# The slot softmax of a gated-slot attention: eight biased exponentials with their row sums, in place of one exponential over a shifted copy

## The reference, cut to what matters

```
z  = cumlogsumexp(s);  g = exp(z_prev - z);  p = exp(s - z)
hk = hk * g + k (x) p          ok = q . hk      # 64 slot scores per token and head
pv = softmax(ok, axis=-1)                       # over the 64 slots: the part that is changed
hv = hv * g + p (x) v          ov = pv . hv
o  = ov * rsqrt(mean(ov^2) + 1e-5) * g_norm_weight * silu(gate);  out = o @ Wo
```

## Time and profile before

| | |
|---|---|
| median of three runs | 2185.8 us |
| the profiled execution's own time | 2185.81 us |
| its span (first to last instruction) | 2184.1 us |
| TensorE (PE) matrix products busy | 2024.7 us, 93% of the span |
| VectorE (DVE) busy | 1399.1 us, 64% |
| ScalarE (ACT) busy | 671.1 us, 31% |
| GpSimd (POOL) busy | 282.9 us, 13% |
| mean granted TensorE clock | 0.976 of full speed |

### The profile page before, as it was taken

The page is one execution under the profiler, slowest core; times in us unless marked ns, Lnnn a source line. Parts: engine busy times, 40 slices in busy tenths (PEclk is TensorE's granted clock), DMA queues, the critical chain, the costliest instruction groups (busy, mean ns, idle before and its releaser), DMA issues. The chain is left out here.

```text
span 2184.1 us, 30684 instructions
## 1 busy us (share of the span) xinstructions
PE 2024.7 (93%) x11728; PEld 1665.3 (76%) x11728; DVE 1399.1 (64%) x2579; ACT 671.1 (31%) x1156; POOL 282.9 (13%) x243
## 2 busy tenths in 40 slices
PE   0999999969999999999999999999998489999996
PEld 0888888857887878878878878788877368888885
DVE  6665656767666666666666666666677556665666
ACT  2443444534121121212221221212221134443443
POOL 4000000131021020120110110201111220000004
PEclk9999999979999999999999999999999689999999
DMA  5433334430010010000100100100001152432336
GB/s 205 142 122 101 132 104 142 145 121 23 1 37 8 1 38 8 18 28 1 37 9 1 37 8 1 37 8 18 20 1 39 58 145 94 136 126 96 126 126 241
DMA packets 46932, 149.61 MB, mean 69 GB/s; under 512 B 5856, under 2 KB 5856, under 8 KB 46816
## 3 DMA queue, kind: packets, MB, share of 16 engines
q1 hardware_dynamic: 38544, 121.13, 17.2%
q0 software_dynamic: 8272, 26.76, 3.7%
HBM read 125.83 MB, written 22.04 MB: 68 GB/s over the span
## 5 line engine op out<-in xcount | busy, mean ns | idle before, releaser
L1154 PE MATMUL at_pj<-at_w_lo,at_xT_hi 128*128 128x512 f32 x512 | 209.7, 410 | 0.0
L1154 PE MATMUL at_pj<-at_w_hi,at_xT_hi 128*128 128x512 f32 x512 | 201.4, 393 | 0.0
L1154 PE MATMUL at_pj<-at_w_hi,at_xT_lo 128*128 128x512 f32 x512 | 200.4, 391 | 0.0
L1128 PE MATMUL at_pj<-at_xT_hi,at_w_lo 128*128 128x512 f32 x384 | 160.4, 418 | 12.2 <-issue 11.5
L503 DVE TENSOR_TENSOR first_ff_w_lo<-first_ff_stage,first_ff_w_hi 128x1024 fp32r<-128x1024 f32 x80 | 98.0, 1226 | 100.7 <-ACT first_ff_w_hi L365 100.7
L503 DVE TENSOR_TENSOR last_ff_w_lo<-last_ff_stage,last_ff_w_hi 128x1024 fp32r<-128x1024 f32 x80 | 98.0, 1224 | 96.8 <-ACT last_ff_w_hi L365 96.5
L1128 PE MATMUL at_pj<-at_xT_lo,at_w_hi 128*128 128x512 f32 x384 | 153.1, 399 | 0.0
L1128 PE MATMUL at_pj<-at_xT_hi,at_w_hi 128*128 128x512 f32 x384 | 153.0, 398 | 0.0
L773 POOL TENSOR_TENSOR at_coef<-at_ms,minus_half 128x4 f32<-128x4 f32 x64 | 63.6, 1010 | 558.5 <-DVE at_ms L1088 558.5
L749 POOL TENSOR_TENSOR at_w_lo<-at_stage,at_w_hi 128x1024 fp32r<-128x1024 f32 (+1 forms) x36 | 78.5, 2180 | 396.7 <-ACT at_w_hi L813 396.7
L1108 DVE TENSOR_TENSOR xres<-at_r,xres 128x512 f32<-128x512 f32 x128 | 88.2, 689 | 64.8 <-PE at_r L1308 64.1
(11 more groups left out here) (284 smaller groups left out, 4774.6 us busy)
## 6 DMA issues: line engine op xcount, KB each, us to landing
first_ff_stage<-wff SPq DMA_DIRECT2D x80, 512.0 KB, 3.3
last_ff_stage<-wff SPq DMA_DIRECT2D x80, 512.0 KB
at_stage<-watt SPq DMA_DIRECT2D x24, 512.0 KB, 3.6
at_stage<-watt SPq DMA_DIRECT2D x16, 384.0 KB, 3.3
xres<-x SPq DMA_DIRECT2D x4, 1024.0 KB, 10.1
first_ff_xg<-sorted_rows SPq DMA_DIRECT2D x4, 1024.0 KB, 7.2
slot_rows<-first_ff_y POOLq DMA_DIRECT2D x4, 1024.0 KB, 5.3
last_ff_xg<-sorted_rows SPq DMA_DIRECT2D x4, 1024.0 KB, 8.2
```

The costliest lines, as they stand in the source:

```text
L1128: last = pe.matmul(PJ[(7 * k + part) % 2][:, :], wq(w, kk, part), x[:, kk, tok], start=(kk == 0 and n == 0), stop=(kk == KC - 1 and n == 2))
L1154: last = pe.matmul(PJ[(7 * k + 3 + t) % 2][:, :], x[:, kk, tok], wvg(w, kk), start=(kk == 0 and n == 0), stop=(kk == KC - 1 and n == 2))
```

## The change

VectorE scales the scores by -1/z instead of 1/z, takes the minimum of each group of 64 columns (minus the maximum of the true scores), and stops there: the shifted copy and the sum of the exponentials are removed. ScalarE does the exponential as eight operations of 64 columns. Each reads the transposed scores in bank `R[5]` with scale -1 and the group's minimum as bias (a pointer to one value for each row), writes to `pv`, and gives the row sum of its output to one column of `den` (`accum_out`). Only the last one signals `pv_done`. ScalarE has one more wait, for `eps_done` of the unit before (L1050, the last reader of `den`). The tile `ok` is kept: other steps use it as room.

```diff
+ lowest = sb("at_lowest", [P, 2 * UC])          # in the place of at_highest
 ScalarE:
- act.wait_ge(ok_shifted, count(i, k, 1, 1))
- act.activation(pv[:, :, :], ok[:, :, :], ACT.Exp).then_inc(pv_done, 1)
+ act.wait_ge(lowest_done, count(i, k, 1, 1))
+ act.wait_ge(eps_done, count(i, k, 1, 0))
+ for cc in range(UC):
+     for h in range(2):
+         n = 2 * cc + h
+         exp = act.activation(pv[:, cc, h * M:(h + 1) * M], R[5][:, cc * P + h * M:cc * P + (h + 1) * M], ACT.Exp,
+                              bias=lowest[:, n:n + 1], scale=-1.0, accum_out=den[:, h * UC + cc:h * UC + cc + 1])
+ exp.then_inc(pv_done, 1)
 VectorE:
- dve.tensor_tensor(okT[:, :], R[2][:, :], rzT[:, :], ALU.mult).then_inc(ok_scaled, 1)
+ dve.scalar_tensor_tensor(out=okT[:, :], in0=R[2][:, :], scalar=-1.0, in1=rzT[:, :], op0=ALU.mult, op1=ALU.mult).then_inc(ok_scaled, 1)
- dve.tensor_reduce(highest[:, :], by_head(turned_ok), op=ALU.max, axis=AX.X).then_inc(highest_done, 1)
- dve.wait_ge(highest_done, count(i, k, 1, 1))
- dve.tensor_tensor(by_head(ok[:, :, :]), by_head(turned_ok), spread(highest), ALU.subtract).then_inc(ok_shifted, 1)
+ dve.tensor_reduce(lowest[:, :], by_head(turned_ok), op=ALU.min, axis=AX.X).then_inc(lowest_done, 1)
- dve.wait_ge(pv_done, count(i, k, 1, 1))
- dve.tensor_reduce(den[:, :], pv[:, :, :].rearrange("p a (h m) -> p h a m", h=2), op=ALU.add, axis=AX.X).then_inc(den_done, 1)
- dve.wait_ge(den_done, count(i, k, 1, 1))
+ dve.wait_ge(pv_done, count(i, k, 1, 1))        # ahead of L1050
```

More of the change, by code:

```diff
@@ L665, in phase_attention @@
         uT_lo = sb("at_uT_lo", [P, 2, 2, 2 * P], F32R)
-        highest = sb("at_highest", [P, 2 * UC])
+        lowest = sb("at_lowest", [P, 2 * UC])
         den = sb("at_den", [P, 2 * UC])
@@ L707, in phase_attention @@
         a_mm, a_masked = sem("at_a_mm"), sem("at_a_masked")
-        ok_mm, ok_scaled, highest_done, ok_shifted = sem("at_ok_mm"), sem("at_ok_scaled"), sem("at_highest_done"), sem("at_ok_shifted")
-        pv_done, den_done = sem("at_pv_done"), sem("at_den_done")
+        ok_mm, ok_scaled, lowest_done = sem("at_ok_mm"), sem("at_ok_scaled"), sem("at_lowest_done")
+        pv_done = sem("at_pv_done")
         ok_tr, p_tr, p_out = sem("at_ok_tr"), sem("at_p_tr"), sem("at_p_out")
@@ L904, in _ @@
         def _(dve):
-            for s in (k_out, s_clipped, z_done, gate_done, kn_out, rz_done, hk_done, a_masked, ok_scaled, highest_done, ok_shifted,
-                      den_done, p_out, b_masked, hv_done, ss_done, eps_done, ms_done, u_done, u_lo, added):
+            for s in (k_out, s_clipped, z_done, gate_done, kn_out, rz_done, hk_done, a_masked, ok_scaled, lowest_done,
+                      p_out, b_masked, hv_done, ss_done, eps_done, ms_done, u_done, u_lo, added):
                 dve.sem_inc(s, 1)
@@ L1032, in pair @@
                     dve.wait_ge(rz_done, count(i, k, 1, 1))
-                    dve.tensor_tensor(okT[:, :], R[2][:, :], rzT[:, :], ALU.mult).then_inc(ok_scaled, 1)
+                    dve.scalar_tensor_tensor(out=okT[:, :], in0=R[2][:, :], scalar=-1.0, in1=rzT[:, :], op0=ALU.mult, op1=ALU.mult).then_inc(ok_scaled, 1)
                     by_head = lambda x: x.rearrange("p a (h m) -> p (a h) m", h=2)
                     turned_ok = R[5][:, :].rearrange("p (a b) -> p a b", a=UC)
-                    spread = lambda x: x[:, :].rearrange("p (a b) -> p a b", b=1).to_broadcast([P, 2 * UC, M])
                     dve.wait_ge(ok_tr, count(i, k, 1, 0))
-                    dve.tensor_reduce(highest[:, :], by_head(turned_ok), op=ALU.max, axis=AX.X).then_inc(highest_done, 1)
-                    dve.wait_ge(highest_done, count(i, k, 1, 1))
-                    dve.tensor_tensor(by_head(ok[:, :, :]), by_head(turned_ok), spread(highest), ALU.subtract).then_inc(ok_shifted, 1)
+                    dve.tensor_reduce(lowest[:, :], by_head(turned_ok), op=ALU.min, axis=AX.X).then_inc(lowest_done, 1)
                     if more:
                         s_clip(i, k + 1)
-                    dve.wait_ge(pv_done, count(i, k, 1, 1))
-                    dve.tensor_reduce(den[:, :], pv[:, :, :].rearrange("p a (h m) -> p h a m", h=2), op=ALU.add, axis=AX.X).then_inc(den_done, 1)
                     dve.wait_ge(p_tr, count(i, k, 1, 0))
```

## The result

The changed kernel takes 2211.2 us in the median of five runs (2202.7 to 2212.2), the kernel before 2185.8 us. The ratio is 1.0103 with a 95% interval of 1.008 to 1.0126: it is slower by 25 us, where 66 were forecast. (The ratio is taken over all executions; the quotient of the medians alone is 1.0116.) Two of the twelve executions of experiment 7, at 2848.7 and 4420.6 us, stood outside the usual spread and are left out of its time and ratio. The profiled execution took 2211.44 us with a span of 2209.8 us, 25.7 us more than before.

The account below looks back on a forecast made before the run. TensorE, busy 93% of the span, was taken as the bound. 56.4 us of its waits in 31 units plus 2.0 in the last gave 58.4; 2185.8 + 58.4 + 8 for the clock = 2252 us, range 2204 to 2286.

Parts of the forecast that it names:

- TensorE is the bound and VectorE's relief is worth nothing: Softmax: 31 of 32 hidden behind TensorE's projections; the 44 us taken off VectorE lie in its idle time, nothing gained.
- The duration of one exponential, 0.309 us: ScalarE's 64-column exponential from PSUM: 222 ns plus 87 ns for the pointer as bias, together 309 ns.
- its bare pace, 0.21: ScalarE's successive biased exponentials without row sum: neighbours overlap by 0.10 us, so 0.21 us for each operation.
- The row sum: ScalarE's row-sum reading behind each exponential, the unknown: pace taken as 0.41 us, eight take 3.38 us.
- between: ScalarE's row sum, middle case: reading waits for its exponential, next exponential overlaps the reading by 0.10 us; pace 0.41.
- nearly free: Rival on ScalarE's row sum: it adds little, pace between 0.21 and 0.31 us, 2193 to 2213 us; chance 0.22.
- The room, 1.56 us: Time from the first exponential's possible start until it would delay TensorE's load for the transposes of pv: 1.56 us.
- The clock, 8 us: TensorE's new pauses make the granted clock fall behind one in six: 5 falls by 1.6 us, 8 us.
- The upper price of the clock: TensorE's clock falling behind one in three of the new pauses: 18 us.
- the bare unit: Last softmax, not hidden behind projections: maximum's end to exponential's end goes from 1.39 to 3.41 us, 2.0 us more.
- What the profile would show: Eight exponentials with readings, 3.4 us; transposes' load waiting in 32 units, 58 us; units 1.8 us longer; some clock falls.
- TensorE's wait is there and the time isn't longer by its sum: Sign at the transposes of pv that would prove the prediction wrong: TensorE waits, but time does not grow by those waits.

Follow-up runs that it names:

- experiment 7: Changed kernel with the first 6 of 12 products of project_vg(.., 1) put ahead of the transposes of pv: 2188.2 us, ratio 1.0019.
- Experiment 5: Kernel before without VectorE's 32 sums of the exponentials, their tile filled once at the start: 2183.6 us, ratio 0.9998.
- experiment 1: Changed kernel with its eight biased exponentials but without the row sum on ScalarE; VectorE sums each unit again: 2184.7 us, ratio 1.0002.
- experiment 6: Kernel before with its one exponential cut into eight of 64 columns from the shifted copy, without bias or row sum: 2195.2 us, one run.
- experiment 3: Kernel before with eight exponentials from the shifted copy, without bias, with row sums, and no sum on VectorE: 2219.7 us, one run.
- experiment 4: Changed kernel with four more biased exponentials with row sums in each unit, written to spare room: 2245.1 us, ratio 1.0273.
- Experiment 2: Changed kernel with the first 3 of 12 products of project_vg(.., 1) put ahead of the transposes of pv: 2188.1 us, ratio 1.0017.
- 9: Changed kernel with 6 products of project_vg(.., 1) ahead of the transposes in the looped pairs, 3 in the last pair: 2188.4 us, ratio 1.0016.
- experiment 10: Changed kernel with six more biased exponentials with row sums in each unit, written to spare room: 2302.5 us, ratio 1.0525.

## Why the prediction was right or wrong, step by step

**TensorE is the bound and VectorE's relief is worth nothing: right.** Experiment 5 shows it for the sum (L1044), experiment 1 for the shifted copy (L1040), and the looped units of experiment 7 (both gone, the exponentials covered, 37.0 us as before) for the two together.

**The duration of one exponential, 0.309 us, and its bare pace, 0.21: right.** 0.31 and 0.206 were measured.

**The row sum: the step that failed.** The prediction took "between", a pace of 0.41 us, by this reasoning: "the reading waits for the exponential, the next exponential overlaps the reading by the usual 0.10". The second half holds, the first does not. The reading overlaps its exponential too. The pace is 0.29, and the eight take 2.47 us, not 3.38. This mis-sized term is 0.91 us a unit, 28 us of the 41 us that the forecast was too high. The rival "nearly free" (chance 0.22), worked out with VectorE's 0.08 us, gave a pace of 0.29, 2.42 us and 2213 us; it was the case that came. That it lies within 2 us of the measured time is partly luck: its room was 0.17 us too small and its eight 0.05 us too short, and what it put past the room was 0.86 us, where the units show 0.74. The row of the other engine had the right price, and the row of the same engine was read as a duration where its share of the pace was wanted: 0.204 less the overlap of 0.10 would have given 0.31.

**The room, 1.56 us: too small by 0.17.** It was taken to TensorE's weight load. Experiment 1 shows that a load 0.22 us late costs nothing. The units give the true room. The end of ScalarE's last operation is counted from the start of the reduction. One number, 2.46 us, is fitted; a unit is longer than before by what that end exceeds it (worked out from the timelines; the last column is the mean of the 23 units without a turn less the 36.97 us of the kernel before):

```
kernel                     end, us   less 2.46   unit less 36.97
experiment 1 (no sum)       2.48       0.02       0.02
experiment 6 (eight bare)   2.73       0.27       0.28
changed kernel              3.20       0.74       0.74
experiment 3 (no bias)      3.47       1.01       1.01
experiment 4 (twelve)       4.38       1.92       1.92
```

So what the exponentials outlast the room by reaches the time one to one. Experiment 2 fits as well: 3.20 against 2.46 + 0.69 leaves 0.05, and its mean is 0.06 above. From the reduction's end the room is 2.46 - 0.69 = 1.77 us, so from the first exponential 1.73, not 1.56. That is 5 us over 31 units.

**The clock, 8 us: wrong.** No fall follows the changed kernel's pauses (0.53 us idle), nor the 1.7 us of experiment 4. The forecast had read a rate of two in six off the turns of the loop and applied half of it. The rate isn't carried over by halves: it was none of 23 at 1.7 us and 20 of 23 at 2.3 us. Nor does the length alone decide: at the turns in the kernel before, the clock fell behind pauses of 1.83 and 2.05 us and not behind 2.08 and 2.10. (The upper price of the clock, 18 us at one in three, is also a little high in itself: a third of 31 pauses at 1.6 us is 16 to 17.)

**The sum.** 28 for the pace, 5 for the room, 8 for the clock and 0.9 for the bare unit (2.0 forecast, 1.1 measured) make 42 us; forecast and measured time are 41 us apart.

**What the profile would show:** the eight with readings of 0.20 us, the wait in all 32 units and the 44 us off VectorE came. The eight took 2.47 us instead of 3.4, VectorE's idle time ahead of pT grew to 2.7 us instead of over 3, the load's wait was 33.1 us instead of 58, the unit 0.7 us longer instead of 1.8, and no stretch at a lower clock stands behind the waits. "TensorE's wait is there and the time isn't longer by its sum" came true in small: 33.1 us of waiting loads cost 24 us, since 0.2 us of each wait is free and 2.6 us stood in the bare unit before.

No version beats the kernel before. Experiment 1, which gives up the row sums, comes back to its time, and experiments 2, 7 and 9, which keep them, come within 0.2% of it. With nothing to win from VectorE none of the runs points to a gain.

## What to carry to other kernels

When a step hidden behind a bound engine is cut into many short ones, what counts is their pace, duration less overlap, times their number, against the cover; work out the cover first, and an operation off an engine that waits anyway is worth nothing. A second instruction that an option brings (here the reading of a row sum) is a count of its own: price it by its share of the pace, not by its duration. Where the cover is short, moving three of the next products ahead of the waiting step gave back about five sixths of the loss without touching the step itself.

## What the runs showed of the hardware that was not expected

- A row sum on ScalarE is an instruction of its own of 0.19 to 0.24 us that adds only 0.083 us (with a pointer as bias, from PSUM) or 0.09 us (without, from SBUF) to the pace, since it overlaps the exponential ahead of it and the one behind it by 0.10 us each.
- TensorE's idle time of 1.7 us in each of 31 units left the clock up; 2.3 us brought it down to 1.2 GHz (a granted clock of 0.51) behind 20 of 23 pauses, about 1.5 us lost each time, and 2.9 us behind 18 of 23. The eight pauses without a fall all belong to the first or second unit of a pair. Why these were spared stays open. The six more exponentials of experiment 10 cost 91 us over the changed kernel, of which their own time is only 56.
- A weight load that came 0.22 us late, while the product of 512 columns ahead still ran, delayed nothing: units of 36.99 us against 36.97.
